# A new slot layout for a step of attention and feed-forward work: contexts of two groups at once, first rows from two DMA queues, layer 1's weights converted on ACT

## The reference

```python
xn = (x - mean(x)) / sqrt(var(x) + 1e-5)                     # per token
q, k, v = (split_heads(xn @ w.T * s + b) for w, s, b in ...) # 16 heads of 8
ctx = softmax(q @ k.T / sqrt(8)) @ v                         # per head, 256 x 256 scores
attn = merge_heads(ctx) @ w_o.T * s_o + b_o
h = s0 * (concat([xn, -xn]) @ pm(k0)); h = relu(h) * 2       # 512 features; pm: True -> 1, False -> -1
h = s1 * (h @ pm(k1));                 h = relu(h) * 2       # 512 features
out = x + attn + s2 * (h @ pm(k2))                           # 128
```

## Time and profile before

| what | us |
|---|---|
| median of 3 runs | 333.4 (333.23 to 333.51) |
| the profiled execution, its own time | 330.62 |
| its span in the trace | 328.8 |
| PE busy | 291.4 |
| DVE busy | 251.9 |
| ACT busy | 223.1 |
| POOL busy | 118.4 |
| mean granted clock of PE | 0.972 of full speed |

### The profile page before, as it was taken

How to read it: one execution, slowest core, us unless ns; L and a number is a source line. 1 busy time by engine, 2 the same in 40 slices (tenths; PEclk the granted TensorE clock), 3 DMA queues, 4 the chain that set the end, 5 groups by cost and what they waited for, 6 DMA issues and landing times.

```text
span 328.8 us, 8642 instructions
## 1 busy us (share of the span) xinstructions
PE 291.4 (89%) x3252; PEld 181.4 (55%) x3252; DVE 251.9 (77%) x388; ACT 223.1 (68%) x339; POOL 118.4 (36%) x253
## 2 busy tenths in 40 slices
PE   6296899999999999999999999999999999989762
PEld 6184555565655656565656556565656565554321
DVE  4727886888878897978888788979788887787622
ACT  3204285878686777868786877777687868675780
POOL 3323343534433343535344333334353444211100
PEclk9679999999999999999999999999999999997997
DMA  4221213021312222121212122121222130210000
GB/s 115 65 72 32 83 26 92 20 84 50 86 34 68 67 54 79 32 73 54 82 50 85 37 79 56 53 80 40 63 53 80 52 85 22 64 52 3 17 19 16
DMA packets 24772, 18.69 MB, mean 57 GB/s; under 512 B 4668, under 2 KB 22556, under 8 KB 24732
## 3 DMA queue, kind: packets, MB, share of 16 engines
q1 hardware_dynamic: 24732, 18.15, 19.7%
HBM read 11.28 MB, written 6.29 MB: 53 GB/s over the span
## 4 chain that ended last, share of the span: by engine, by line
PE 77%; ACT 9%; issue 6%; DVE 6%; POOL 1%; POOLq 0%; ACTq 0%; DVEq 0%
PE ctx_bank L842 20%; PE work L865 19%; PE st_pair L817 10%; PE s_pair L831 7%; PE work L894 5%; PE work L872 5%; PE work L858 4%; ACT probs L511 3%; PE work L946 3%; PE st_pair L879 2%; PE work L933 2%; ACT xT L569 2%; DVE neg_max L622 2%; ACT xT_hi L569 1%; ACT qk L520 1%
## 5 line engine op out<-in xcount | busy, mean ns | idle before, releaser
L622 DVE TENSOR_REDUCE neg_max<-s_pair 128x4 f32<-128x1024 f32 x124 | 150.7, 1215 | 39.6 <-PE s_pair L831 37.7
L511 ACT ACTIVATE probs<-st_pair,exp_scale 128x1024 f32<-128x1024 f32 x124 | 138.4, 1116 | 41.6 <-PE st_pair L817 41.5
L842 PE MATMUL ctx_bank<-probs,v_ext 128*32 128x256 f32 x1024 | 69.5, 388 | 6.9 <-issue 3.8
L865 PE MATMUL work<-r_hi,w 128*128 128x256 f16 x256 | 60.4, 276 | 3.8 <-DVE w L761 2.1
L500 ACT ACTIVATE r_hi<-work 128x512 f16<-128x512 f32 x64 | 36.5, 593 | 35.5 <-PE work L865 29.5
L865 PE MATMUL work<-r_lo,w 128*128 128x256 f16 x256 | 60.0, 275 | 0.0
L817 PE MATMUL st_pair<-q_rows,k_rows 34*128 34x256 f16 x496 | 48.8, 275 | 8.2 <-ACT probs L511 7.4
L463 POOL TENSOR_SCALAR max_down<-neg_max 128x16 f32<-128x16 f32 x32 | 8.2, 256 | 128.5 <-DVE neg_max L622 128.5
L596 DVE SCALAR_TENSOR_TENSOR r_lo<-work,r_hi 128x512 f16<-128x512 f32 x64 | 42.3, 680 | 7.6 <-ACT r_hi L500 7.6
L831 PE MATMUL s_pair<-k_rows,q_rows 34*128 34x256 f16 x496 | 47.9, 271 | 0.2 <-DVE neg_max L622 0.2
L842 PEld LDWEIGHTS ctx_bank<-probs,v_ext 128*32 128x32 f32 x1024 | 29.3, 109 | 31.7 <-issue 18.9
(11 more groups left out here) (100 smaller groups left out, 353.4 us busy)
## 6 DMA issues: line engine op xcount, KB each, us to landing
k_rows<-k_scratch SPq DMA_DIRECT2D x64, 64.0 KB
q_rows<-q_scratch SPq DMA_DIRECT2D x32, 128.0 KB
xin<-x SPq DMA_DIRECT2D x16, 128.0 KB, 2.2
k_scratch<-qk_part SPq DMA_DIRECT2D x32, 64.0 KB, 2.1
q_scratch<-qk_part SPq DMA_DIRECT2D x32, 64.0 KB, 2.1
out<-outs SPq DMA_DIRECT2D x16, 128.0 KB, 1.9
q_rows<-max_rows SPq DMA_DIRECT2D x64, 4.0 KB
q_rows<-zeros SPq DMA_DIRECT2D x32, 8.0 KB
```

The source lines that it names most:

```text
L511: nc.scalar.activation(probs[j // 2 % 2][:, j % 2 * 2:j % 2 * 2 + 2, :, :].rearrange("p h k q -> p (h k q)"), pairs[j % len(pairs)][:, :], ...
L622: nc.vector.tensor_reduce(out=neg_max[:, j // QUARTER, :, j % QUARTER, :], in_=pairs[j % len(pairs)][:, :].rearrange("p (x q k) -> p x q k ...
L842: last = mm(ctx_bank[VC * j:VC * (j + 1), g % 2 * SEQ:(g % 2 + 1) * SEQ], v_ext[s.par(lag)][:, kt, GROUP * g + j, :], probs[g % 2][:, j, k ...
L865: last = mm(b[:, (m % 2) * SEQ:(m % 2 + 1) * SEQ], w1[:, kk, m * P:(m + 1) * P], part[:, kk, :], start=kk == n == 0, stop=kk == FB - 1 and ...
```

## The change

What it does to each part:

- **Layout.** There is one more step in front and one behind (FIRST_STEP -2, LAST_STEP 19). Inputs are loaded at lag -2 and outputs stored at lag 4. q, k and their cast move from lag 0, slot 0 to lag -1, slots 5 to 7. Layer 0 is cut into slots 2 and 3. Layer 1's blocks stand in slots 6, 7 and 7, and the last one in slot 0 of the next step. Layer 2 is one piece in slot 2; v and the transposes of xn move to slot 3, the output projection to slot 6, the statistics of the next batch to slots 0 and 1. Work on POOL and DMAs on SP are put in a new order too.
- **Slots of PE.** A slot is now `scores_for_max(j)`, other work, `scores_for_exp(j + 1)`; the group 0 of a batch's exponentials stands at the end of slot 7 of the step before.
- **Contexts.** Two groups at once, in slot 4 (lag 2) and slot 1 (lag 3); `probs` has four buffers for it instead of two.
- **Transposed maxima.** `max_part` is padded with zeros to 128 columns, and all of it is transposed.
- **Work banks** are shared out anew.
- **First batch.** Its q stores and q row loads are issued on ACT, the k ones on SP. Layer 1's weights are converted on ACT (two activations of 1024 columns) in step -1. 6 warming transposes stand before q and k of batch 0 and 4 before step 1, in place of the 30.

The diff, cut to its core (POOL's and SP's reordering in part):

```diff
-WARM_START, WARM_FIRST_STEP = 16, 30
+FIRST_STEP, LAST_STEP = -2, BATCH + 3
+WARM_START, WARM_QK, WARM_ROWS = 16, 6, 4
-BANK = {"qk": 0, "l0b": 0, "l1a": 0, "l0a": 1, "l1b": 1, "max1": 2, "l2": 2, "max0": 2, "o": 2}
+WORK = {"l0a": 0, "max0": 0, "o": 0,
+        "l0b": 1, "qk": 1, "l1b": 1,
+        "max1": 2, "l2": 2, "v": 2, "xT": 2, "l1a": 2}
...
-        probs = [sb(f"probs{n}", [P, GROUP, TT, SEQ], f32) for n in range(2)]
+        probs = [sb(f"probs{n}", [P, GROUP, TT, SEQ], f32) for n in range(GROUPS)]
...
+        def store_q(s, eng, part, ready, stored):
+            s.wait(eng, ready, 1, -1, 1)
+            eng.dma_start(q_scratch[:, part], qk_part[:, part, 0, :]).then_inc(stored, 16)
+        def load_q_rows(s, eng, lag):
+            s.wait(eng, hi_stored, 32, lag, 32)
+            s.wait(eng, lo_stored, 32, lag, 32)
+            for par in range(2):
...
@@ SP's step @@
+                if s.has(1):
                     s.wait(sp, max_rows_ready, 2, 1, 1)
                     store_max(s, 1, 0)
+                if s.has(-1):
+                    s.wait(sp, rows_loaded, LOADS, 0, LOADS)
+                    for part, ready, stored in ((0, hi_ready, hi_stored), (1, lo_ready, lo_stored)):
+                        s.wait(sp, ready, 1, -1, 1)
+                        sp.dma_start(k_scratch[:, part], qk_part[:, part, 1, :]).then_inc(stored, 16)
+                        if s.first != -1:
+                            store_q(s, sp, part, ready, stored)
+                if s.has(1):
+                    s.wait(sp, max_rows_ready, 2, 1, 2)
+                    store_max(s, 1, 1)
+                if s.has(-1):
+                    if s.first != -1:
+                        zero_q_rows(s)
+                    load_k_rows(s, 0, hi_stored)
+                if s.has(4):
+                    # the out DMA
+                if s.has(-1):
+                    if s.first != -1:
+                        load_q_rows(s, sp, -1)
+                    load_k_rows(s, 1, lo_stored)
@@ POOL's step @@
+ order: split_xT (0), split_max (2, 1), split_qk (0), normalisation (-1),
+        [first step: zeros of max_part and v_ext], y (2), residual (0), ctxn (3), split_max (1, 0)
@@ ACT's step @@
+                    if j == 0 and s.has(1):   # relu_hi of l1b, waits for l1_psum and l2_psum
+                    if j == 0 and s.has(2):
                         copy_max(s, 2, 1)
+                    if j == 2 and s.has(0):   # relu_hi of l0a;  j == 3: of l0b
+                    if j == 2 and s.has(1):   # ffn
+                    if j == 4 and s.has(-1):  # xT, xT_hi
+                    if j == 4 and s.first == 0:
+                        load_q_rows(s, act, 0)
+                    if j == 4 and s.has(1):   # v_ext;  then ctxT for lag 3
+                    if j == 5 and s.has(1):
+                        copy_max(s, 1, 0)
+                    if j == 6 and s.has(-1):  # scales q and k
+                    if j == 6 and s.first == -1:
+                        second_layer_weights(0)
+                        store_q(s, act, 0, hi_ready, hi_stored)
+                        store_q(s, act, 1, lo_ready, lo_stored)
+                        second_layer_weights(1)
+                    if j == 7 and s.has(0):   # relu_hi of l1a
+            def second_layer_weights(half):
+                act.wait_ge(signs_ready, 1)
+                act.wait_ge(ffn_weights_loaded, 16 * N_FFN_DMAS)
+                blocks = slice(half * FB // 2, (half + 1) * FB // 2)
+                nc.scalar.activation(w1[:, blocks, :]..., k1_sb[:, blocks, :]..., ACT.Identity,
+                                     scale=sgn[:, 5:6], bias=sgn[:, 6:7]).then_inc(w1_ready, 1)
@@ DVE's step, behind the reduction of each slot @@
+ j 0: token_stats (-1);  1: relu_lo l1b (1), moments (-1), turn_context (3, 1);  2: reciprocal (3)
+ j 3: relu_lo l0a (0);  4: ctx_back (3), relu_lo l0b (0);  5: turn_context (2, 0);  6: outs (3)
+ j 7: cast of q and k (-1), relu_lo l1a (0)
@@ PE @@
-            def context(s, lag, g):
-                s.wait(pe, probs_ready, HALF, lag, 2 * (g + 1))
-                s.wait(pe, ctx_turned, 2, lag, g // 2)
+            def context(s, lag, half):
+                s.wait(pe, probs_ready, HALF, lag, QUARTER * (half + 1))
+                s.wait(pe, ctx_turned, 2, lag, half)
...
+                for g in range(2 * half, 2 * half + 2):
...
-                nc.tensor.transpose(b[0:2 * HROWS, 0:P],
-                                    max_part[:, half].rearrange("p x r h t -> p (x r h t)"), ident16[:, :]
+                nc.tensor.transpose(b[:, 0:P], max_part[half][:, :], ident16[:, :]).then_inc(maxT_psum, 1)
@@ PE's step: each slot @@
-                    if s.has(2):
-                        scores_for_exp(s, j)
                     if s.has(1):
                         scores_for_max(s, j)
+ j 0: layer1_block l1b 3 (lag 1), max_to_rows (2, 1);  1: context (3, 1);  2: layer0 a, layer 2 whole (lag 1)
+ j 3: layer0 b, v (lag 1), xT (lag -1) [first: keep_warm(6)];  4: context (2, 0)
+ j 5: max_to_rows (1, 0), q and k (lag -1);  6: output projection (3), layer1_block l1a 0
+ j 7: layer1_block l1a 1, l1b 2 [step 0: keep_warm(4)]
+                    if j == HALF - 1 and s.has(1):
+                        scores_for_exp(s, 1, 0)
+                    if j < HALF - 1 and s.has(2):
+                        scores_for_exp(s, 2, j + 1)
```

More of the change, by code:

```diff
@@ L405, in step @@
             def step(s):
+                if s.has(0) and s.first != 0:
+                    split_xT(s, nc.gpsimd, pool, 0)
                 if s.has(2):
@@ L921, in step @@
+                    if j == 3 and s.first == -1:
+                        pe.wait_ge(most_ready, 1)
+                        mm(work[0][:, 2:3], ones_f32[:, :], most_qk[:, :], start=True, stop=True
+                           ).then_inc(most_psum, 1)
+                        keep_warm(WARM_QK)
                     if j == 4 and s.has(2):
-                        context(s, 2, 1)
-                    if j == 4 and s.has(1):
+                        context(s, 2, 0)
+                    if j == 5 and s.has(1):
@@ L924, in step @@
                         max_to_rows(s, 1, 0)
-                    if j == 4 and s.has(0):
-                        layer1_block(psum("l1a"), 1).then_inc(l1_psum, 1)
-                    if j == 5 and s.has(0):
-                        layer1_block(take_bank(s, "l1b"), 2)
-                    if j == 5 and s.has(3):
+                    if j == 5 and s.has(-1):
+                        b = take_bank(s, "qk")
+                        s.wait(pe, xT_copied, 2, -1, 2)
+                        for n in range(2):
+                            last = mm(b[:, n * SEQ:(n + 1) * SEQ], w_sb[:, n, :], xT[s.par(-1)][:, :],
+                                      start=True, stop=True)
+                        last.then_inc(qk_psum, 1)
```

446 lines of the change are left out of this document (208 added, 238 removed).

## The result

The changed kernel takes 310.5 us (median of 4 runs, 306.8 to 311.2) against 333.3 us (332.99 to 333.51). The ratio is 0.929, 95% interval 0.922 to 0.937. The forecast was 317.5 us with a range of 313.5 to 325: the sign was right, the size too small.

The account below looks back on a forecast made before the run. PE was taken to bound the kernel. Steps -12.5, head -4.7 and tail +1.3 us made -15.9, so 333.4 became 317.5 us, with a range of 313.5 to 325 for 8 in 10.

Parts of the forecast that it names:

- Steady step: One of 14 repeated pipeline steps: from 18.04 to about 17.15 us, -12.5 us in all; bounds 16.8 and 18.04.
- The slot list: PE time estimated for each of the new step's eight slots, from 1.57 to 2.42 us.
- the other sum: Step from totals: 17.21 us of PE work, less 0.40 for grouping, plus 0.36 for floors, 17.17 us.
- PE's work: PE work in a step, found as the step less 0.83 us of stalls: 17.21 us, after grouping 16.81.
- The floor: Shortest slot, set by DVE's reduction from the single s_pair bank: 1.84 us; slots 0 and 5 lengthened by 0.36 together.
- Change of kind: Switching between kinds of matmul on PE costs about 0.10 us; grouped contexts save four per step, -0.40 us.
- The evacuations keep up: In the steady step DVE and ACT finish their work in time; four of the covers are under 0.5 us.
- The head: Start of the kernel: first maxima at 22.4 for 25.5 us (-3.1), first step with maxima -1.6; together -4.7 us.
- The tail: End of the kernel: contexts of two groups cost +1.3 us, bounds +0.5 and +2.5, with PE's clock unchanged.
- ACT's conversions: In the head, converting layer 1's weights on ACT costs nothing; one conversion about 1.12 us, bounded by half or twice.
- The second queue: In the head, issuing on ACT too saves at most 2.4 us of SP's issues; nothing in the time.
- The rivals: Half the stalls return, 323.8 us (0.19); only ends change, 330.0 (0.06); slower, waiting for rows (0.05); first maxima unmoved, 320.6.

Follow-up runs that it names:

- e7: Changed kernel with 7 of the 8 matmuls of layer 1's block in slot 0 left out; 309.1 us, one run.
- e9: Changed kernel with one small transpose between the two context groups in slot 1, in steps 4 to 15; 315.8 us, one run.
- e5: Changed kernel with the contexts one group at a time again, the rest of the layout kept; 327.5 us.
- e6: Kernel before the change with only the contexts of two groups in slots 1 and 4 and four probs buffers; 348.4 us.
- e1: Changed kernel with POOL's zeroing of v_ext moved from step -1 to step 0; 307.2 us.
- e4: Changed kernel with the v_ext zeroing moved to step 0, 20 warming transposes in the head and more in the tail's waits; 303.7 us.
- e8: e4 with 17 more warming transposes in step 1, 18 more in the last steps, and the last batch's third context issued earlier; 299.2 us.
- e11: Changed kernel with layer 1's weights converted on DVE, behind its split of batch 0's q and k; 311.5 us.
- e10: Changed kernel with the first batch's q stores and q row loads back on SP's queue; 309.0 us.
- e12: e8 with the first batch's q stores and q row loads back on SP's queue; 301.0 us.

## Why the prediction was wrong

Three of its terms lie outside their own bounds: the step (16.36, at best 16.8), the first maxima (25.83, at worst 24.5) and the tail (+4.7, at worst +2.5). That the time was only 7 us off is in part luck, since the step brought more and the ends less.

- **What bounds the kernel: right.** PE's own work sets the step; its share of the steps rose to 99%.
- **Steady step: the term that failed.** Forecast 17.15 (0.89 less), measured 16.36 to 16.43. In the working stand two sums, and they did not agree. The slot list, 1.57 + 2.42 + 2.1 + 1.9 + 2.42 + 1.75 + 2.0 + 2.37, is 16.53, with the floors 16.89; the other sum (17.21 - 0.40 + 0.36) is 17.17, and I took it. Against the list the measured slots are 1.70 and 1.70 for the two floors (0.28 less), 1.98 and 1.75 for slots 2 and 3 (0.27 less), and 0.1 more in slots 6 and 7. Together 0.46 less than the list. Choosing the other sum cost 0.28 more. So the step that failed is PE's work of 16.81 us with its 0.36 us of floors; slot by slot it measured 16.25 and 0.18.
- **The floor** was read at a place where something else stood in it. The group at 167.20 came 0.21 us behind an exp group that had itself waited for ACT, while the reduction had ended at 167.01. That is a distance of groups and not the reduction's own limit; the limit is 1.70 (e7: 0.42 us to DVE's start, 1.22 of reduction, 0.06 to the next group).
- **PE's work** was found by taking the stalls from the step, and so each stall that I missed was counted as work. PE's timeline of the kernel before shows two of them:

```profile
153.65 0.38 PE L831 MATMUL s_pair<-k_rows,q_rows 34*128 34x256 f16 x4
154.28 0.64 PE L842 MATMUL ctx_bank<-probs,v_ext 128*32 128x256 f32 x8 [0.24 <-issue]
...
162.71 0.38 PE L831 MATMUL s_pair<-k_rows,q_rows 34*128 34x256 f16 x4
163.15 0.64 PE L842 MATMUL ctx_bank<-probs,v_ext 128*32 128x256 f32 x8
```

  Other work follows a maxima group after 0.31 us; here it is 0.63 and 0.44. The waits list names the first alone. I make the stalls some 1.05 us a step, in place of 0.83. Layer 2 in two halves took 0.55 + 0.60, whole it takes 0.99, which the forecast had at its old cost. The work was put too high by 0.56 us (16.81 against 16.43 less some 0.18 us of floor waits); these two are 0.38 of it, 0.18 I can't place.
- **Change of kind, 0.10 us: right** (e9: 0.12). The grouping's worth of 0.40 is near e5's 0.48; e6 shows that it is not had by itself.
- **The evacuations keep up: right.** No wait is listed for PE in the steps. That this was no matter of course e5 and e6 show, with 0.7 and 1.4 us of waits a step.
- **The head: wrong, -1.65 for -4.7.** First maxima 25.83 for 22.4; the step behind them, 13.67 for 13.9, was right. xn of batch 1 reached PE at 17.76 for 15.1, because DVE was free only at 14.68, where the walk had 12.2. Two things are missing there. One is the zeroing beside DVE's xn, for which the walk has no term: 1.30 us (e1). The other is the rate of PE at batch 0's q and k: "costs some 0.3 us" rests on before, where they ran at full rate; in e4, at full rate too and without the zeroing, DVE is free at 11.38, 0.8 ahead of the walk, and e1 at half rate is 2.0 us behind e4. Then the clock again: q and k of batch 1 took 1.84 us for 2.1, start to start, but the 24 records of layer 1 took 4.20 in place of 3.5, since the clock stayed at 1.2 GHz until about 24 us, not 20. Without all three the first maxima start at 19.73 (e4).
- **The tail: wrong, +4.7 for +1.3,** and the term that failed is PE's clock, "I take it as unchanged". Two contexts of 32 records ran at 1.2 GHz, 3.64 us each for 1.93: 3.4 us. The rest, 4.7 - 3.4, is the 1.3 that the contexts of two groups were to cost. That this is more than a fit of two numbers no run shows: before's tail had slow records too (a context of 16 records at 297.87 took 1.93 us in place of 1.07), so the net loss to the clock is under 3.4, and what the grouping costs there stays open. And e8, which kept the clock and drew the third context forward, ends at 34.7, 0.3 below before's tail.
- **ACT's conversions: right** that their time is hidden (2 x 1.24 us, e11). **The second queue:** the forecast gave it nothing, and the runs agree within their spread (e10, e12).
- **The rivals:** none came true. No PE wait for max_rows stands in the steps.

The profiled execution by its terms: 330.62 - 1.65 - 23.6 + 4.7 = 310.1 us, as measured. So of the 7 us between forecast and median, 11.1 us are the step, of which 6.5 were lost again in head and tail (3.05 + 3.45), and 2.4 us are the distance of the profiled run to the median: 2.8 before, 0.4 after.

## What to carry to other kernels

A strict rotation of slots is read from the distances between its pace-setting groups, in one whole step; price the new layout slot by slot, and where this sum and the one from totals disagree, find the reason before choosing. Group matmuls of one kind only together with a new spread of the evacuations: here the spread alone brought 0.2 us of 1.7 a step, and the grouping alone cost 0.6. At the ends look at what the other engines do beside the first link of the chain, and at the rate of PE's own records where it will have gaps, since the clock column can miss a slow beginning.

## What the runs showed of the hardware

- Two small DVE operations from SBUF to SBUF beside POOL's two memsets of 128x1024: 2.20 us in place of 0.60 (after, e1). One conversion of 512 columns beside them: 1.96 in place of 0.42 (e1, after).
- A change between matmuls that fill the array and context matmuls of 32 columns costs 0.12 us (e9).
- The same tail code took 39.8 and 37.3 us in two kernels that differ only in the head (after, e1); one context at 1.2 in place of 2.4 GHz is 1.7 us of it.
- A longer time at 2.4 GHz in the head does not keep it: e4's clock was 1.00 up to the first maxima and 0.89 in the stretch behind them, where PE waits for r_lo; with 17 more transposes there (e8) it was 1.00. The same program can do either: e9 fell to 0.89 where after stood at 1.00.
- Six warming transposes and batch 0's q and k ran at half rate in after (1.52 and 1.91 us) and at full rate in e4 (0.85 and 1.03), with 1.00 as the profile's clock in both.
- Converting 1024 columns of uint8 to float16 takes 1.24 us on ACT and 1.53 / 2 = 0.8 on DVE (e11).
